# Attention values as 32-column weights over scaled probabilities, scores in two row groups

## The reference

```python
scores = jnp.einsum('bhqd,bhkd->bhqk', q, k) * scale + bias
attn = jax.nn.softmax(scores, axis=-1)
out = jnp.einsum('bhqk,bhkd->bhqd', attn, v)
out = out.transpose(0, 2, 1, 3).reshape(B, S, D)
return jnp.einsum('bsd,ed->bse', out, Wo)
```

## Time and profile before

| | |
|---|---|
| median of 3 runs | 269.38 us (269.06 to 269.48) |
| profiled execution | 269.51 us, span 267.7 us |
| TensorE granted clock, mean | 0.992 |
| TensorE busy | 243.5 us (91%), 1562 products and transposes |
| VectorE busy | 177.8 us (66%) |
| ScalarE busy | 119.2 us (45%) |
| GpSimd busy | 69.4 us (26%) |
| bytes moved | 26.11 MB, mean 98 GB/s |

### The profile page before, as it was taken

The page is one execution under the profiler, slowest core; times in us unless marked ns, Lnnn a source line. Parts: engine busy times, 40 slices in busy tenths (PEclk is TensorE's granted clock), DMA queues, the critical chain, the costliest instruction groups (busy, mean ns, idle before and its releaser), DMA issues.

```text
span 267.7 us, 4160 instructions
## 1 busy us (share of the span) xinstructions
PE 243.5 (91%) x1562; PEld 217.0 (81%) x1562; DVE 177.8 (66%) x376; ACT 119.2 (45%) x205; POOL 69.4 (26%) x74
## 2 busy tenths in 40 slices
PE   1988989999989999988977999999889989999991
PEld 2978989998979999777966998787658968998880
DVE  2545882696984997477767486997378556348463
ACT  4525745435175372273714599761363214541000
POOL 4011120212123023011661343797400010340010
PEclk9999999999999999999997999999999999999999
DMA  6999768775534020200020002252000000000010
GB/s 200 394 396 402 232 176 307 240 254 157 169 90 155 2 73 5 82 0 0 4 78 0 2 0 80 81 142 94 0 2 0 0 0 2 0 2 0 21 39 20
DMA packets 8851, 26.11 MB, mean 98 GB/s; under 512 B 1400, under 2 KB 3200, under 8 KB 8576
## 3 DMA queue, kind: packets, MB, share of 16 engines
q1 hardware_dynamic: 8832, 25.86, 28.6%
HBM read 25.33 MB, written 0.52 MB: 97 GB/s over the span
## 4 chain that ended last, share of the span: by engine, by line
PE 74%; DVE 8%; ACT 7%; issue 6%; DMA 2%; SPq 1%; POOL 1%; POOLq 0%; DVEq 0%; ACTq 0%
PE ps L627 68%; PE ps L630 6%; DMA raw<-in_ctx 2%; DVE prob L1137 1%; SPq L353 1%; POOL rstd L408 1%; DVE mx L1136 1%; DVE Z L950 1%; ACT prob L550 1%; DVE on L1149 1%; ACT raw L478 1%; ACT L611 1%; ACT kblk L542 1%; DVE kblk L1191 1%; ACT L598 0%
## 5 line engine op out<-in xcount | busy, mean ns | idle before, releaser
L627 PE MATMUL ps<-ch 128*128 128x130 f32 (+1 forms) x208 | 53.6, 274 | 5.5 <-ACT ch L507 5.4
L627 PE MATMUL ps<-ch,cl 128*128 128x260 f32 (+1 forms) x208 | 53.3, 317 | 0.0
L627 PE MATMUL ps<-w,hT 128*128 128x512 f32 x192 | 47.3, 401 | 0.0
L627 PEld LDWEIGHTS ps<-ch 128*128 128x128 f32 (+1 forms) x208 | 41.2, 198 | 6.3 <-ACT ch L507 5.3
L627 PEld LDWEIGHTS ps<-w,hT 128*128 128x128 f32 x192 | 35.7, 188 | 8.9 <-issue 0.5
L627 PEld LDWEIGHTS ps<-ch,cl 128*128 128x128 f32 (+1 forms) x208 | 41.0, 197 | 0.4 <-issue 0.2
L1051 DVE TENSOR_TENSOR cl<-raw,ch 128x1024 fp32r<-128x1024 f32 (+1 forms) x31 | 30.8, 1025 | 7.5 <-ACT ch L514 7.3
L514 ACT ACTIVATE ch<-raw 128x1024 fp32r<-128x1024 f32 (+1 forms) x31 | 26.3, 887 | 14.2 <-DMA raw<-in_ctx 8.3
L408 POOL TENSOR_TENSOR rstd<-ve,half_exp 128x2 f32<-128x2 f32 (+1 forms) x14 | 9.5, 678 | 78.3 <-DVE ve L922 78.2
L627 PE MATMUL ps<-xHL,dense 128*128 128x256 f32 x192 | 25.8, 295 | 1.5 <-DVE xHL L1200 1.5
L627 PEld LDWEIGHTS ps<-xHL,dense 128*128 128x128 f32 x192 | 24.8, 200 | 2.0 <-DVE xHL L1200 1.8
(11 more groups left out here) (162 smaller groups left out, 422.7 us busy)
## 6 DMA issues: line engine op xcount, KB each, us to landing
raw<-in_ctx SPq DMA_DIRECT2D x23, 512.0 KB, 4.3
raw<-in_w SPq DMA_DIRECT2D x8, 512.0 KB, 3.6
w<-in_w SPq DMA_DIRECT2D x2, 1024.0 KB, 9.8
stage<-in_dense SPq DMA_DIRECT2D x4, 512.0 KB, 5.8
mask<-in_mask SPq DMA_DIRECT2D x1, 800.5 KB, 9.2
rows<-in_rows SPq DMA_DIRECT2D x1, 768.0 KB, 7.9
raw<-in_ctx SPq DMA_DIRECT2D x8, 65.0 KB
raw<-in_ctx SPq DMA_DIRECT2D x4, 128.0 KB, 2.5
```

The source lines that it names most:

```text
L627: return pe.matmul(o, l, r, start=start, stop=stop, skip_group_check=not check)
```

## The change

The scores are cut into products of 64 rows: for each j, each sequence and each half g of the feature rows, the weights are `qp` rows of that half and the moving operand is `kblk`, now with two blocks of 64 keys instead of four. Half g writes bank `tile_bank(i) + g`.

After the exponential, the new VectorE step `shares` computes sums and reciprocals and multiplies the probabilities by them in place; `turn_p` waits for `shares`. `values` then exchanges its operands: weights are `vz`, 64 keys by 32 columns of which 16 are the values of a head and 16 are zero, the moving operand is `probT`, 64 keys by 64 queries. For each j there are two accumulated passes over the parity hl of the head, each over four column groups r and two sequences bb, 32 products in all; each writes 32 partitions of PSUM, and sequence bb reads the rows of its half and writes bank `tile_bank(i) + bb`. The result stands transposed already: ScalarE copies it to `aT` (one copy), and the steps `sums`, the normalisation into `on`, and `turn_o` with its four transposes and two VectorE operations are gone. All four lists of the plan are newly ordered.

```diff
@@ second_half_steps
+        ("norm1", 1), ("hidden_product", 0), ("hidden_product", 1), ("hidden_product", 2), ("hidden_product", 3),
+        ("gates", 0), ("gate_groups", 0), ("turn_z", (1, 0)), ("gate_experts", 0), ("hidden", 0),
+        ("proj1_product", 1), ("hidden", 1), ("hidden", 2), ("proj1", 1), ("piece", 5), ("gate_best", 0),
+        ("score_product", 4), ("piece", 6), ("hidden_product", 4), ("score", 4), ("hidden_product", 5), ("hidden", 3),
+        ("piece", 7), ("hidden", 4), ("hidden_product", 6), ("shares", 4), ("score_product", 5),
+        ("hidden_product", 7), ("shared_product", 0), ("turn_p", 4), ("hidden", 5), ("score", 5), ("hidden", 6),
+        ("shared_product", 1), ("hidden", 7), ("piece", 8), ("piece", 9), ("shared", 0), ("shares", 5), ("shared", 1),
+        ("piece", 10), ("experts_product", (0, 0)), ("turn_p", 5), ("values", 4), ("values", 5), ("experts", (0, 0)),
+        ("project", 4), ("project", 5), ("experts_product", (0, 1)), ("experts_product", (0, 2)), ("piece", 11),
+        ("norm2", 1), ("turn_z", (1, 1)), ("experts", (0, 1)), ("piece", 12), ("experts", (0, 2)), ("proj2", 1),
+        ("experts_product", (0, 3)), ("score_product", 6), ("experts", (0, 3)), ("experts_product", (1, 0)),
+        ("score", 6), ("shares", 6), ("experts_product", (1, 1)), ("score_product", 7), ("turn_p", 6),
+        ("experts_product", (1, 2)), ("score", 7), ("shares", 7), ("turn_p", 7), ("values", 6), ("experts", (1, 0)),
+        ("values", 7), ("project", 6), ("project", 7), ("experts_product", (1, 3)), ("rms1", 1), ("experts", (1, 1)),
+        ("experts", (1, 2)), ("turn_x", 1), ("experts", (1, 3)),
@@ first_half_steps
+        ("xo_product", 0), ("gram", 15), ("cross2_product", 4), ("gram", 16), ("xo", 0), ("norm1", 0), ("split", 17),
+        ("turn_z", (0, 0)), ("split", 18), ("split", 19), ("piece", 1), ("proj1_product", 0), ("proj1", 0),
+        ("piece", 2), ("score_product", 0), ("gram", 17), ("piece", 3), ("cross2", 4), ("evac", 5), ("score", 0),
+        ("cross3", 4), ("gram", 18), ("shares", 0), ("score_product", 1), ("cross4", 4), ("turn_p", 0), ("gram", 19),
+        ("score", 1), ("cross1", 5), ("shares", 1), ("cross2_product", 5), ("split", 20), ("turn_p", 1),
+        ("values", 0), ("cross2", 5), ("values", 1), ("project", 0), ("project", 1), ("norm2", 0), ("cross3", 5),
+        ("gram", 20), ("split", 21), ("split", 22), ("evac", 6), ("turn_z", (0, 1)), ("split", 23), ("cross4", 5),
+        ("cross1", 6), ("proj2", 0), ("cross2_product", 6), ("gram", 21), ("cross2", 6), ("score_product", 2),
+        ("gram", 22), ("piece", 4), ("score", 2), ("cross3", 6), ("gram", 23), ("shares", 2), ("evac", 7),
+        ("score_product", 3), ("cross4", 6), ("turn_p", 2), ("score", 3), ("cross1", 7), ("cross2_product", 7),
+        ("shares", 3), ("turn_p", 3), ("values", 2), ("cross2", 7), ("values", 3), ("project", 2), ("cross3", 7),
+        ("project", 3), ("cross4", 7), ("xo_product", 1), ("rms1", 0), ("turn_x", 0), ("xo", 1),
...
-    kblk, _ = place("kblk", [P, KC * BH, 4, S])
-    vblk, _ = place("vblk", [P, TH, H // 2, 2, 2 * HD])
+    kblk, _ = place("kblk", [P, KC * BH, 2, S])
+    vz, _ = place("vz", [P, TH, H // 2, 2, 2 * HD])
...
+                elif step == "values":
+                    act.wait_ge(sem("pv"), i + 1)
+                    copy(aT[i % 2][:, :, :, :].rearrange("p j b q -> p b j q"),
+                         ps[:, tile_bank(i):tile_bank(i) + 2, 0:P].rearrange("p b (j q) -> p b j q", j=KC), "aT")
...
-                            last = mm(ps[:, tile_bank(i) + j, :].rearrange("p (r b k) -> p r b k", b=2, k=S)[:, :, bb, :],
-                                      qp[:, jb, :, :].rearrange("p h q -> p (h q)"), kblk[:, jb, :, :], True, True)
+                            for g in range(2):
+                                dims = slice(g * P // 2, (g + 1) * P // 2)
+                                got = ps[:, tile_bank(i) + g, :].rearrange("p (j r b k) -> p j r b k", j=KC, b=2, k=S)
+                                last = mm(got[:, j, :, bb, :], qp[dims, jb, :, :].rearrange("p h q -> p (h q)"), kblk[dims, jb, :, :],
+                                          True, True)
...
-                    for c in range(H // 2):
-                        last = mm(ps[:, tile_bank(i), c * 4 * HD:(c + 1) * 4 * HD], probT[:, i % 2, c, :],
-                                  vblk[:, i % 2, c, :, :].rearrange("p b d -> p (b d)"), True, True)
+                    spots = [(r, bb) for r in range(4) for bb in range(2)]
+                    for j in range(KC):
+                        for hl in range(2):
+                            for r, bb in spots:
+                                keys = slice(bb * S, bb * S + S)
+                                last = mm(ps[32 * r:32 * r + 32, tile_bank(i) + bb, j * S:(j + 1) * S], vz[keys, i % 2, 4 * j + r, hl, :],
+                                          probT[keys, i % 2, 4 * (r // 2) + 2 * j + r % 2, hl * S:(hl + 1) * S], hl == 0, hl == 1)
...
-                elif step == "sums":
+                elif step == "shares":
                     k = i % 2
+                    rows_of = prob[:, k, :, :].rearrange("p c (b k) -> p (c b) k", b=2)
                     dve.wait_ge(sem("prob"), i + 1)
-                    link(dve.tensor_reduce(sm[:, k, :], prob[:, k, :, :].rearrange("p c (b k) -> p (c b) k", b=2), AX.X, ALU.add))
+                    link(dve.tensor_reduce(sm[:, k, :], rows_of, AX.X, ALU.add))
                     link(dve.reciprocal(rs[:, k, :], sm[:, k, :]))
...
+                    dve.tensor_tensor(rows_of, rows_of, rs[:, k, :].unsqueeze(2).to_broadcast([P, H, S]),
+                                      ALU.mult).then_inc(sem("shares"), 1)
```

More of the change, by code:

```diff
@@ L112, in first_half_steps @@
-        ("evac", 6), ("values", 0), ("values", 1), ("cross3", 5), ("turn_o", 0), ("turn_o", 1), ("piece", 1),
-        ("cross4", 5), ("cross1", 6), ("project", 0), ("project", 1), ("norm2", 0), ("gram", 21), ("gram", 22),
-        ("split", 23), ("turn_z", (0, 1)), ("cross2_product", 6), ("cross2", 6), ("proj2", 0), ("gram", 23),
-        ("cross3", 6), ("evac", 7), ("score_product", 2), ("score", 2), ("cross4", 6), ("cross1", 7),
-        ("score_product", 3), ("turn_p", 2), ("score", 3), ("piece", 2), ("cross2_product", 7), ("sums", 2),
@@ L132, in second_half_steps @@
-        ("piece", 8), ("turn_p", 5), ("sums", 5), ("shared", 0), ("shared", 1), ("experts", (0, 0)), ("values", 4),
-        ("values", 5), ("piece", 9), ("turn_o", 4), ("turn_o", 5), ("piece", 10), ("project", 4), ("project", 5),
-        ("experts_product", (0, 1)), ("experts_product", (0, 2)), ("piece", 11), ("norm2", 1), ("experts", (0, 1)),
-        ("turn_z", (1, 1)), ("piece", 12), ("experts", (0, 2)), ("proj2", 1), ("experts_product", (0, 3)),
-        ("score_product", 6), ("experts", (0, 3)), ("score", 6), ("score_product", 7), ("experts_product", (1, 0)),
@@ L578, in _ @@
                         q = slice(32 * r, 32 * r + 32)
-                        last = act.activation(kblk[q, :, r, :], kcos[q, :, :], ACT.Copy)
+                        last = act.activation(kblk[q, :, r % 2, :], kcos[q, :, :], ACT.Copy)
                     last.then_inc(sem("kblk"), 1)
```

102 lines of the change are left out of this document (29 added, 73 removed).

## The result

The changed kernel takes 277.21 us (median of 4 runs, 276.14 to 278.49); the kernel before, run on the same chip, takes 269.43 (269.06 to 269.57). The ratio is 1.029, 95% interval 1.024 to 1.035: slower, where 268.0 had been forecast, and just outside the range of 260 to 277. The profiled execution took 278.49 us, with a span of 276.7.

What follows compares the result with a forecast made beforehand. TensorE, busy 91% of the span, was taken to bound the kernel. From 269.5 us, -14.1 (TensorE's work) + 10.7 (waits before `turn_p`) - 1.9 (tail) + 3.8 (other moved steps) = -1.5 gave 268.0 us; range 260 to 277.

Steps and rivals of the forecast that it cites:

- Scores, V, `turn_o` and changes of division: TensorE's attention work: scores -6.6, second transpose -3.5, values -6.9, changes of array division +2.9, in all -14.1 us.
- eight tiles at once: Rival for `values`: all eight array tiles work side by side and changes of tiling are free; 261.5 us, chance 24%.
- the row halves: Rival for `values`: only the two row halves overlap, weight loads going one behind another; 275.2 us, chance 24%.
- the instruction floor: Rival for `values`: an instruction pair can't issue faster than about 0.11 us; 318 us, chance 6%.
- scores that don't overlap: Rival for scores: the 64-row halves do not run side by side, 6.6 us more; 274.6 us, chance 4%.
- An entry and leaving: Changing the array's division: entry 0.2 us for scores, about 0.13 for small weights, leaving 0.1; 2.9 us over twelve stays.
- The rule of the Trainium skill (TensorEngine Tiling, section Key Properties): Any tiling-mode change drains TensorE, so leaving costs as much as entering; 4.1 us by it alone, sum 1.2 us worse.
- Waits for the longer way to `turn_p`: TensorE waits while `shares` precedes the transpose of the probabilities: 12.3 us against 1.6 before, so +10.7.
- The third pair: Third pair of scores: `hidden` 7 stands behind the second causal score on VectorE and `experts_product` (0,0) needs it; about 3.5 us.
- Tail: End of attention: waits for `on` and `aT` (0.9 + 0.5) and five restarts of 0.1 go; -1.9 us.
- restarts: End of attention: five TensorE restarts of 0.1 us, weights not loaded ahead, go away.
- Other steps that the order moves: Added waits for `xHL`, for `ctxT`, for the norm before `turn_z` (0,0), and four small ones put at 0.1; +3.8 us.

Runs made afterwards that it cites:

- `e10_no_multiply_old_order`: All new steps in the order of the kernel before, without multiplying the probabilities by the reciprocal sums (attention not normalised): 261.89 us, ratio 0.969.
- `e5_no_multiply`: The changed kernel, new order kept, without multiplying the probabilities by the reciprocal sums (attention not normalised): 270.51 us, ratio 1.002.
- `e4_old_steps_new_order`: The products, sums and `turn_o` of the kernel before, laid along the new order of steps: 290.99 us, ratio 1.082.
- `e13_scores_two_moves`: The kernel before with 64-row scores alone, plus `cross2_product` 7 and `experts_product` (0,0) each moved ahead of a `turn_p`: three runs 280.3 to 281.8 us, one 270.7.
- the three filled kernels: The changed kernel with useless products in TensorE's wait before `experts_product` (0,0): eight, 279.63 us; four, 276.27; four plus two before `hidden_product` 8, 274.75.
- `e1_scores`: The kernel before, in its own order and with its V path, only the score products split into 64-row halves: 266.42 us, ratio 0.988.
- `e9_filled_half`: The changed kernel with four useless products laid into TensorE's wait for `hT` before `experts_product` (0,0): 276.27 us, ratio 1.021.
- `e8_sums_on_tensor`: The kernel before, old order, with new scores and V products, sums taken by TensorE with weights of ones, division after `values`: 271.12 us, ratio 1.009.
- `e3_new_steps_old_order`: All new steps in the order of the kernel before, `shares` standing where `sums` stood: 301.67 us, ratio 1.124.
- `e12_shares_after_score`: All new steps in the order of the kernel before, with `shares` directly behind its `score` on VectorE: 293.42 us, ratio 1.088.

## Why the prediction was wrong

The sum was -1.5 us; the spans differ by +9.0. First what the runs show as a whole, by medians: the new products bring -7.9 us (`e10_no_multiply_old_order` against before), the new order without the multiplication costs 8.6 (`e5_no_multiply` against `e10_no_multiply_old_order`), and the multiplication in the new order 6.7. That is +7.4, where +7.8 was measured. The steps of the forecast that failed are the other waits that the order brings, which it set too low (3.8 us for 7.2), and the falls of the clock, which it did not price (4.4 us). By its own steps, from the profiled executions:

- **Scores, V, `turn_o` and changes of division: -14.1 forecast, about -16 measured.** By start-to-start times -16.4, from which some 0.4 for four entries goes off, since it shows in the step before (`turn_p` 1 now takes 1.02 us, 100.38 to 101.40, instead of 0.9). A pair of `values` takes 1.68 us, 1.8 forecast; a score 1.09, where 0.9 and its changes were forecast. Right, and slightly too careful. The rivals of eight tiles at once (0.9 us a pair), of the row halves (3.6), of the instruction floor (some 14) and of scores that don't overlap fall. An entry and leaving together show as 1.09 - 0.90 = 0.19 us in a score, and 0.1 in the step before. The rule of the Trainium skill (TensorEngine Tiling, section Key Properties) is that a change of tiling mode drains TensorE; if leaving so costs as much as entering, the two are 0.4 us by the prediction's rows, and the trace shows at most 0.3.
- **Waits for the longer way to `turn_p`: 12.3 forecast, 12.7 measured.** By pairs 2.8, 1.8, 5.4 and 2.7 against 3.5, 3.0, 3.5 and 2.3 (the waits for `prob`, `gs` and `hT` in each pair). That the total is so near is in part luck. Only 4.9 us is listed as waiting for `prob`, where the forecast said 10 or more; `hT` 4.8 and `gs` 2.4 stay in `e5_no_multiply`, and 4.5 and 2.7 in `e4_old_steps_new_order`, so more than half of the 12.7 comes from the order and not from the multiplication. The third pair was mis-sized: the forecast named `hidden` 7 behind the second causal score rightly, but counted only VectorE's queue and not the table load and exponential on ScalarE (2.34 us) nor POOL's 1.42 behind them.
- **Tail: -1.9 forecast, -1.4 shown.** No wait for `on` or `aT` is left. The 0.5 for restarts can't be read from the traces.
- **Other steps that the order moves: +3.8 forecast, +7.2 measured.** This is the term that was mis-sized most. Over before: `xHL` +2.3 us (1.5 forecast); the norm before `turn_z` (0,0), in the row `Z` L939, 1.3 (1.4 forecast); `zT` +1.2, `kblk` +1.1 and `mb` -0.5, which had been set at 0.1 together; `cl` 0.8 in the opening, which had been put at nothing; small ones for the rest.
- **Not priced at all: the clock.** TensorE at its lower level costs 1.7 us in `proj1_product` 1, 2.7 behind the wait for `hT` and 1.5 in the closing stretch, 5.9 in all; before has one such fall in its first `hidden_product` steps, 1.5 us (60 instructions in 8.88 us, 7.36 in `e13_scores_two_moves` at the full clock). Net +4.4. Only of the second of these is it shown, by the three filled kernels, that it goes with the wait ahead of it.
- **The opening: TensorE reaches its full speed later**, which differs from run to run (below). For 3.7 us more it takes 0.86 us for four products that then take 0.47, by estimate 1.7 us.

Together: -16 + 11.1 (12.7 less the 1.6 of before) - 1.4 + 7.2 + 4.4 + 1.7 = 7.0, against 9.0. A listed wait counts from the end of a product, and the next could have started 0.2 us before that end (175.72 in the kernel after, where the filling starts at 175.52). With 28 waits listed after and 21 before, that is some 1.4 more by estimate; the last 0.6 is open.

No rival came true, though two named nearly the same time (275.2 and 274.6) by mechanisms that the traces exclude. `e10_no_multiply_old_order` and `e1_scores` show the same from the other side: where the new products bring little extra waiting, they gain 1 to 3%.

## What to carry over

A cheaper product on the busiest engine is worth what the other engines' chain leaves of it: before a step such as a normalisation is put ahead of a product, lay out every queue that its result, and each result queued behind it, must pass through (here VectorE, ScalarE with its table load, POOL), for the order as it will be. Price a wait of TensorE like those here (2.2 to 3.8 us) at more than its length, for the products behind it may run at half the clock, though they do not always; and measure each part of a change alone, since here one part (the scores) is a gain of 1.2% that the whole hides. A sequence is only good for the steps it was laid out for: this one costs 21.6 us with the old steps and gives 24.5 with the new ones.

## What the runs showed of the hardware

- **Small products in different tiles start very close.** 128 instructions of 64 rows and 32 weight columns start within 1.68 us, 13 ns each on average, where 0.11 us per instruction was the rate of the old ones.
- **What a wait costs beyond itself.** Waits of 1.6 and 3.8 us were followed by a granted clock of 0.57 over 8 us; the price was 2.7 us, most of the longer wait again. The same wait of 3.8 us in `e5_no_multiply` cost less: the twelve products behind it took 4.47 us, not 5.49. And a wait of 2.2 us was followed by a fall in the kernel after (36 instructions in 6.05 us) and by none in `e9_filled_half` (4.53).
- **The beginning varies.** Products of 260 columns take 0.42 us while TensorE has not reached full speed, and 0.28 after; the granted clock of the records reads 1.00 in both. In the profiled executions this came near 11 us in before and near 15 in after. TensorE's timeline of before, its opening:

```profile
8.75 0.42 PE L627 MATMUL ps<-ch,cl 128*128 128x260 f32 x1
11.69 0.28 PE L627 MATMUL ps<-ch,cl 128*128 128x260 f32 x1
```

The same of after:

```profile
13.27 0.42 PE L628 MATMUL ps<-ch,cl 128*128 128x260 f32 x1
14.86 0.28 PE L628 MATMUL ps<-ch,cl 128*128 128x260 f32 x1
```

Over the profiled executions of this study the first product of 0.28 us started between 8.7 and 15.8 us. A difference of 1 to 2 us between two single executions may be that alone.
- **TensorE can stand still within a long run of small instructions.** After 216 of them it stood 2.1 us with nothing else to wait for (`e8_sums_on_tensor`); in the kernel after, with rows of 128, waits of that kind come to 0.7 us, as in before. The three kernels with such rows in the old order (`e3_new_steps_old_order`, `e10_no_multiply_old_order`, `e12_shares_after_score`) have one more, of 1.6 us, between two `experts_product`, so these waits are not confined to rows of small products. Their cause is not shown.
